# One-hots of destinations in the fourth layer's attention: from one VectorE compare per eight tiles to absolute difference and Relu on ScalarE, pair by pair

## The reference, cut to what matters

```
k_j   = k[src] + e                  # e = edge_attr @ We + be
alpha = einsum('ehc,ehc->eh', q[dst], k_j) / sqrt(64)
ex    = exp(alpha - segment_max(alpha, dst)[dst])
alpha = ex / (segment_sum(ex, dst)[dst] + 1e-16)
out   = segment_sum((v[src] + e) * alpha[..., None], dst) + x @ Ws + bs
```

## Time and profile before

| what | value |
|---|---|
| median of 3 runs | 4554.0 us (4553.05 to 4560.82) |
| profiled execution, its own time | 4529.55 us |
| span of its profile | 4527.8 us |
| busy DVE, PE, POOL, ACT | 2951.7, 3176.2, 2749.4, 1634.9 us |
| `attend(1)`, `attend(2)` | about 2570 to 3468 and 3584 to 4482 us of the span |
| mean granted TensorE clock, whole span | 0.806 |

### The profile page before, as it was taken

How to read it: one execution, slowest core, us unless ns; L and a number is a source line. 1 busy time by engine, 2 the same in 40 slices (tenths; PEclk the granted TensorE clock), 3 DMA queues, 4 the chain that set the end, 5 groups by cost and what they waited for, 6 DMA issues and landing times. The chain is left out here.

```text
span 4527.8 us, 51805 instructions
## 1 busy us (share of the span) xinstructions
PE 3176.2 (70%) x11623; PEld 2181.9 (48%) x11623; DVE 2951.7 (65%) x7240; ACT 1634.9 (36%) x4707; POOL 2749.4 (61%) x2215
## 2 busy tenths in 40 slices
PE   4555553476666853777775788888887878888884
PEld 3444442344444442444443356666564456666662
DVE  3445447344444464666665478888887578888887
ACT  3334444011111221223233245555552145555553
POOL 4666661766665005667760188888881288888881
PEclk7667776688887875556667889999998999999996
DMA  4544443566566203444441599999994599999993
GB/s 134 112 113 111 114 112 84 154 195 198 184 192 183 87 12 116 114 114 113 114 99 52 145 188 192 190 186 191 190 181 107 162 185 192 190 190 186 191 179 85
DMA packets 378970, 660.99 MB, mean 146 GB/s; under 512 B 59010, under 2 KB 161395, under 8 KB 378676
## 3 DMA queue, kind: packets, MB, share of 16 engines
q0 software_dynamic: 190208, 406.78, 47.5%
q1 hardware_dynamic: 184356, 247.08, 17.0%
q10 hardware_dynamic: 4112, 3.83, 0.3%
HBM read 582.15 MB, written 75.33 MB: 145 GB/s over the span
## 5 line engine op out<-in xcount | busy, mean ns | idle before, releaser
L1653 POOL DMA_INDIRECT t_kv<-kv_tab,srcT x880 | 1415.7, 1609 | 648.8 <-ACT t_kv L1779 389.4
L1280 POOL DMA_INDIRECT grow<-h_tab,srcT x440 | 451.2, 1025 | 468.3 <-POOLq L83 276.7
L776 POOL DMA_INDIRECT grow<-x_tab,srcT x440 | 441.1, 1003 | 304.2 <-issue 107.1
L1836 PE MATMUL bank<-t_kv,t_oh 128*128 128x260 f32 x1760 | 555.4, 418 | 99.8 <-DVE acc L1730 66.6
L476 POOL DMA_INDIRECT grow<-h_tab,srcT x440 | 436.2, 991 | 245.2 <-issue 96.6
L1809 PE MATMUL bank<-we,t_aT 128*128 128x256 f32 x1760 | 504.7, 413 | 26.2 <-DMA t_aT<-attrT_tab 25.5
L1820 PE MATMUL bank<-H,t_ohT 128*128 x1760 | 497.4, 409 | 23.0 <-DVE t_ks L1690 22.3
L1778 ACT COPY t_kv<-bank 128x512 f32<-128x512 f32 x440 | 256.3, 582 | 618.6 <-PE bank L1809 583.7
L1796 ACT ACTIVATE t_kv<-t_kv 128x64 f32<-128x64 f32 x1760 | 465.8, 344 | 13.4 <-DVE t_kv L1706 13.4
L824 DVE TENSOR_TENSOR acc<-acc,bank 128x272 f32 x440 | 192.5, 437 | 393.9 <-PE bank L901 151.3
L1836 PEld LDWEIGHTS bank<-t_kv,t_oh 128*128 128x128 f32 x1760 | 318.2, 201 | 258.5 <-ACT t_kv L1796 133.5
(11 more groups left out here) (396 smaller groups left out, 4804.5 us busy)
## 6 DMA issues: line engine op xcount, KB each, us to landing
t_aT<-attrT_tab SPq DMA_DIRECT2D x110, 512.0 KB
lob<-lo_tab SPq DMA_DIRECT2D x110, 256.0 KB
arow<-in_edge_attr SPq DMA_DIRECT2D x440, 64.0 KB
attrT_tab<-aT SPq DMA_DIRECT2D x55, 512.0 KB
t_lob<-lo_tab SPq DMA_DIRECT2D x110, 256.0 KB
grow<-h_tab,srcT POOLq DMA_INDIRECT x880
t_kv<-kv_tab,srcT POOLq DMA_INDIRECT x880
kv_tab<-kv SPq DMA_DIRECT2D x10, 1290.0 KB, 5.2
```

Source lines behind the costliest of these rows:

```text
L776: nc.gpsimd.indirect_dma_start(out=grow[:, t % RA, 0:F], out_offset=None, in_=x_tab, in_offset=bass.IndirectOffsetOnAxis(ap=srcT[:, t:t + ...
L1280: nc.gpsimd.indirect_dma_start(out=grow[:, t % R2, :], out_offset=None, in_=h2_tab, in_offset=bass.IndirectOffsetOnAxis(ap=srcT[:, t:t + 1 ...
L1653: nc.gpsimd.indirect_dma_start(out=kv[:, t % UB, :], out_offset=None, in_=kv_tab, in_offset=bass.IndirectOffsetOnAxis(ap=srcT[:, t:t + 1], ...
L1836: nc.tensor.matmul(PS[4 + t % WIN3][:, 0:LHW], oh[:, t // HB % 2, t % HB, :], kv[:, t % UB, F:KVW], start=True, stop=True).then_inc(produc ...
```

## The change

The compare on DVE goes. ACT makes the one-hots of one pair in each step: for each of the two tiles the absolute difference of the node number and the destination (`Abs(dlocT - iota_n)`, 128x128), a wait for the second of them, then `Relu(1 - x)` over both (128x256), which is 1 where the difference is 0 and 0 elsewhere. It does so one step ahead of the scatter that reads them, behind `fill` and the softmax's Exps and ahead of the weighing of the heads. `oh_ready` now counts pairs, and PE waits for it at every even tile.

```diff
-                        def one_hots(g):
-                            if g >= 2:
-                                dve.wait_ge(products, (g - 1) * HB)
-                            nc.vector.tensor_tensor(oh[:, g % 2, :, :], iota_n[:, :].unsqueeze(1).broadcast_to([P, HB, P]),
-                                                    dlocT[:, g * HB:(g + 1) * HB].unsqueeze(2).broadcast_to([P, HB, P]), ALU.is_equal).then_inc(oh_ready, 1)
...
-                        one_hots(0)
...
-                            if k % 4 == 2 and 0 < (q + 2) // 4 < NH:
-                                one_hots((q + 2) // 4)
...
+                        step = Chain(act, ac)
+
+                        def one_hots(q):
+                            if q >= NB // 2:
+                                act.wait_ge(products, 2 * q + 2 - NB)
+                            pair = oh[:, q // 4 % 2, 2 * q % HB:2 * q % HB + 2, :]
+                            for v in range(2):
+                                last = nc.scalar.activation(pair[:, v, :], iota_n[:, :], ACT.Abs, bias=dlocT[:, 2 * q + v:2 * q + v + 1], scale=-1.0)
+                            step(last)
+                            nc.scalar.activation(pair, pair, ACT.Relu, bias=ones[:, 0:1], scale=-1.0).then_inc(oh_ready, 1)
...
                             if 0 <= b < NBT and k == 2:
                                 sm.act(act, b, 4)
+                            if 0 <= q + 1 < pairs:
+                                one_hots(q + 1)
                             if 0 <= q < pairs:
...
                                 if t % HB == 0:
-                                    pe.wait_ge(oh_ready, t // HB + 1)
                                     pe.wait_ge(msg_ready, t // HB + 1)
+                                if t % 2 == 0:
+                                    pe.wait_ge(oh_ready, q + 1)
                                 pe.wait_ge(act_ready, t + 1)
```

More of the change, by code:

```diff
@@ L1630, in attend @@
             tag = f"t{layer}"
-            names = "lo_in0 lo_in1 lo_in2 at_in0 at_in1 at_in2 oht_ready oh_ready e_ready filled q_ready q_used sums_done msg_ready act_ready products added zeroed dve".split()
+            names = "lo_in0 lo_in1 lo_in2 at_in0 at_in1 at_in2 oht_ready oh_ready e_ready filled q_ready q_used sums_done msg_ready act_ready products added zeroed dve act".split()
             (lo_in0, lo_in1, lo_in2, at_in0, at_in1, at_in2, oht_ready, oh_ready, e_ready, filled, q_ready, q_used, sums_done, msg_ready, act_ready,
-             products, added, zeroed, dv) = [sem(f"{tag}_{n}") for n in names]
+             products, added, zeroed, dv, ac) = [sem(f"{tag}_{n}") for n in names]
             lo_in, at_in = (lo_in0, lo_in1, lo_in2), (at_in0, at_in1, at_in2)
```

## The result

The changed kernel takes 4533.38 us (median of 6 runs, 4523.9 to 4536.35), the kernel before, on the same chips, 4553.52 (6 runs, 4546.91 to 4560.82). The ratio is 0.9953, with a 95% interval of 0.9939 to 0.9967: 20 us faster (15 to 28 by the interval), where 45 were forecast. The sign and the branch "faster" were right, the size was not; the time lies inside the stated range, and nearest to the first rival.

What follows compares the result with a forecast made beforehand. DVE was taken to bound the kernel at 30.97 us a turn (8 pairs). Loop 29.3, ACT 28.5 and POOL 29.95 us made the turn 30.1; 0.87 us in 52 turns, 45 us, takes 4554.0 to 4509 us; range 4486 to 4552.

Steps and rivals of the forecast that it cites:

- the branch "faster": Total time: faster by over 0.2%, chance 0.80.
- the first rival: The loop gains little, through ACT's price, PE's waits or DMA; gathers hold 30.57 us a turn, 21 us gained; chance 0.20.
- DVE bounds the kernel before: Attention phases: DVE, busy 529.6 of 600 us, sets the turn of 30.97 us, POOL close behind.
- the loop could go at 29.3 us: Loop of DVE, PE and ACT: two compares removed save 1.7 us a turn.
- ACT's price: One-hots on ACT: two Abs, a wait and a Relu cost 1.12 us a pair, bounds 1.0 and 1.64.
- ACT's order: ACT's program order: its turn is 28.5 us, PE's product of k = 7 comes 0.4 late, other waits for heads nothing.
- POOL at 29.95 us a turn: Gathers on POOL: 0.62 us a turn of stalls inside the removed compare L1680 goes, from 30.57 us.
- The sum: Turn falls from 30.97 to 30.1 us; 0.87 us in 52 turns gives 45 us.
- the second rival: Nothing gained: DVE waits for PE, whose matmuls run slower after an idle spell; time stays at 4554; chance 0.08.
- The third: Slower: ACT's turn becomes longest; at 1.64 us a pair 31.6 us, 35 us more, 4589; chance 0.12.
- The fourth: A table load beside each Exp on ACT, if Abs or Relu isn't in its table; part of the slower rival.
- Signs named ahead: Profile if right: gathers near 1.88 us apart, mean about 1575 ns; if wrong: PE waiting for ACT's heads at each product.

Runs made afterwards that it cites:

- Run 8: Kernel before with all three long DVE instructions (one-hots, ohT, weighing) in four pieces: 4654.91 us, ratio 1.0236; with only the weighing in four: 4555.36 us, 1.0086.
- Run 3: Changed kernel with ACT's one-hots put ahead of the softmax's Exps instead of behind them: ratio 0.9926 to the kernel before.
- runs 1: Changed kernel with no one-hots made after the first 16 tiles, the scatter using old ones: ratio 0.9925 to the kernel before.
- Run 4: Changed kernel with DVE's weighing of eight tiles cut in four instructions of two tiles: ratio 0.9926 to the kernel before.
- run 5: Changed kernel with both one-hots ahead of the Exps and the weighing in four pieces: 4501.6 us, ratio 0.9902 to the kernel before.
- run 6: One-hots ahead of the Exps and weighing in four pieces, also without the loads of aT after the first three: ratio 0.9889 against 0.9902 with them.
- run 2: Kernel before with ACT's one-hot instructions added into spare memory, DVE still making the real ones: ratio 1.0007.

## Why the prediction was half right

- **DVE bounds the kernel before**: right, by a thin margin. Run 8 shows the bound, and DVE's busy time fell from 529.6 to 496.5 us in 600. That the loop could go at 29.3 us wasn't seen: the shortest turn of any run is 30.0.
- **ACT's price**: right. One-hots took 0.70 + 0.04 + 0.40 = 1.14 us (forecast 1.12), a step 3.04 us (3.02): the Abs 394 ns (386), the Relu 508 ns (494).
- **ACT's order**: the step that failed in part. "What is queued behind the one-hots on ACT is the heads, and PE's product waits for these": I then checked this for k = 7 alone, where I found 0.4 us. At k = 2 all of the one-hots come between the Exp and the heads, PE waits there in 40 of 56 turns (1.36 us in the timeline above), and in 17 of these its matmuls then run at the lower clock and pass up to 2 us on to DVE. Run 3 puts the price at 12 us by ratio, 17 by phases. This wait was a term put at nothing.
- **POOL at 29.95 us a turn**: the other step that failed, "Without it POOL goes at 29.95 us a turn". I took the excess of the gathers inside L1680 as gone with L1680. The stalls of all gathers went from 60.5 to 55.9 us only, 16 gathers take 30.54 us and not 29.95, and the turn is 30.5 to 30.6. The changed kernel and runs 1 and 3 show 55 to 75 gathers inside the weighing where there were 30, with 26 to 30 us. Run 4 removes these stalls and gets 12 us by ratio, 15 by phases; in run 5 the turn is 30.0, the forecast's 30.1. That the gathers fall into step with DVE's long instructions, because one now waits for the other, fits the rows; it wasn't tested by itself.
- **The sum**: 45 us forecast, 20 measured, and 12 + 12 us for the two steps. The version without both has a ratio of 0.9902, which on 4553.5 us is 4509 us; its interval is 12 us to either side, so that it's the forecast's very number is luck. The gain also isn't made up as the sum had it, of a shorter turn in 52 turns: 6.3 of the 19.3 us are the gathers' distance, the rest is DVE no longer falling behind them.
- **Rivals**: the first, little gain, came about, and with its price: it had the gathers hold the turn at 30.57 us and 21 us gained. But it gave other reasons: ACT's price was right, and DMA traffic isn't the bound (run 6). The clock of the second rival is part of what happened. The third is ruled out by the result and run 2. (Its upper price doesn't follow from its own terms, which add up to 1.60 us a pair and not 1.64; nothing hangs on it.) The rule of the Trainium skill that stood beside it, VectorE rather than ScalarE for relu and add (ScalarE: Activation LUTs, "Rules for kernel authors"), would have made the change a loss if ACT had been the bound; the runs show a gain, and ACT had the time (483 of 600 us busy). The fourth, a table load beside each Exp, isn't seen: between Exp and one-hots ACT has no gap.
- **Signs named ahead**: the turn near 1.88 us a gather and a mean of 1575 ns did not come. "PE for ACT's heads at each product" didn't come either: PE's products waited 4.7 us for the heads in the two phases, less than before (16.8), but 54.9 us for the one-hots ahead of them, which no sign had named.

## What to carry to other kernels

A stall that comes from two engines meeting isn't removed with the instruction it was met on. Where the waiting engine becomes the bound, it meets the next long one: count the stall time of all of them, and take off only what a version with all of them shortened shows. When work moves to an engine with idle time, look where in its program order that idle time lies: here it cost 12 to 17 us behind the wait, and nothing ahead of it. And the same edit (shorter DVE instructions) can be a gain or a loss by which engine sets the pace, so ask for it again after each change.

## What the runs showed of the hardware

- A gather issued by POOL that starts while DVE runs a long instruction with two SBUF inputs waits until that ends. Inside the weighing of 2993.13 to 2994.36 it took 2.28 us and ended 1.41 us behind the weighing, where it takes 1.54 us alone; each of the 53 gathers that stalled in the changed kernel's weighings ended 1.41 to 1.43 us behind its one. So it is with the 35 that stalled in the compare for `ohT`, which has one wide input (1.40 to 1.43 us). The lock that the Trainium skill tells of (SBUF — State Buffer, "SBUF: two separate sides") agrees. Shorter instructions lessen it: pieces of 0.42 us cut the loss from 30.3 to 7.3 us.
- DVE's instructions of 256 elements took 0.42 us (two inputs) and 0.37 us (one input), those of 1024 took 1.22 and 0.75. Two compares a turn in quarters were enough to make DVE the bound again.
- PE's stretches at 1.2 GHz cost where another engine waits for it: in the turn of the earlier trace rows the stretch ended ahead of DVE's product and cost nothing, in the changed kernel's turn it cost DVE 1.97 us. They came behind an idle spell of PE of over 1 us in 17 of 40 turns, and in none of the 16 turns without one.
- The DMA share went from 1.04 to 1.00 only when a fifth of the traffic was taken away.
